# A transformer layer whose last three batches are projected beside the attention of the batch in front

## The reference

```
def bitnet_linear(x, weight, scale_param):
    s = jnp.maximum(jnp.mean(jnp.abs(weight), axis=1), 1e-08)
    y = jnp.einsum('bsi,oi->bso', x, jnp.sign(weight / s[:, None]))
    y = y * (s * scale_param)[None, None, :]
    return jnp.nan_to_num(y, nan=0.0, posinf=1000000.0, neginf=-1000000.0)
...
q, k, v = (bitnet_linear(layernorm(x), w, c) for w, c in ...)
attn = softmax(q @ k.T / sqrt(16)); x = x + bitnet_linear(attn @ v, o_weight, o_scale)
...
W = base + mean(abs(w - base)) * sign(w - base)     # for w1, w3 and w2
x = x + (silu(n @ W1.T) * (n @ W3.T)) @ W2.T        # n = layernorm(x)
```

## Time and profile before

| what | value |
|---|---|
| median of three runs | 1074.68 us |
| the profiled execution | 1078.31 us |
| its span, from the first to the last instruction | 1076.5 us |
| PE busy | 955.0 us (89%) |
| DVE busy | 784.5 us (73%) |
| ACT busy | 528.8 us (49%) |
| POOL busy | 132.8 us (12%) |
| mean granted clock of PE | 0.948 of 2.4 GHz |

### The profile page before, as it was taken

How to read it: one execution, slowest core, us unless ns; L and a number is a source line. 1 busy time by engine, 2 the same in 40 slices (tenths; PEclk the granted TensorE clock), 3 DMA queues, 4 the chain that set the end, 5 groups by cost and what they waited for, 6 DMA issues and landing times.

```text
span 1076.5 us, 14793 instructions
## 1 busy us (share of the span) xinstructions
PE 955.0 (89%) x4770; PEld 624.1 (58%) x4770; DVE 784.5 (73%) x1088; ACT 528.8 (49%) x972; POOL 132.8 (12%) x150
## 2 busy tenths in 40 slices
PE   1838348999999999997968999999999999999997
PEld 0727313333333333332445888888888888888886
DVE  6847468999999999996796557864588456864443
ACT  3624206888888888886556332232313332132221
POOL 0204001122111211110000111101101011011110
PEclk9978758999999999997889999999999999999999
DMA  7134324555456544634457200231002400040001
GB/s 253 35 101 164 117 100 122 179 147 145 131 168 170 140 142 143 183 80 142 138 159 238 68 1 1 66 114 60 0 0 78 161 0 0 9 147 1 0 0 39
DMA packets 78962, 106.06 MB, mean 99 GB/s; under 512 B 12960, under 2 KB 36512, under 8 KB 78912
## 3 DMA queue, kind: packets, MB, share of 16 engines
q1 hardware_dynamic: 75360, 101.04, 30.7%
q10 hardware_dynamic: 2688, 2.63, 0.7%
q0 software_dynamic: 864, 1.77, 0.5%
HBM read 76.29 MB, written 28.58 MB: 97 GB/s over the span
## 4 chain that ended last, share of the span: by engine, by line
PE 63%; DVE 14%; SPq 9%; DMA 8%; issue 4%; ACT 1%; POOL 0%; DVEq 0%; ACTq 0%
PE psum L1219 14%; PE psum L1220 14%; PE psum L1221 14%; DVE nmx L861 8%; PE psum L1133 6%; SPq L371 6%; PE psum L1123 6%; PE psum L1107 4%; DMA x_sb<-_attn_hidden_states_dram 2%; DMA factors<-wstat 2%; DVE dsum L947 2%; DMA q_parts<-q_lo 1%; PE psum L1144 1%; PE psum L1209 1%; PE psum L1145 1%
## 5 line engine op out<-in xcount | busy, mean ns | idle before, releaser
L687 ACT ACTIVATE probs<-psum 128x512 f32<-128x512 f32 x512 | 274.3, 602 | 92.5 <-PE psum L1123 91.5
L861 DVE TENSOR_REDUCE nmx<-psum 128x2 f32<-128x1024 f32 x256 | 300.4, 1218 | 26.3 <-PE psum L1107 24.2
L1219 PE MATMUL psum<-fxh,wh 128*128 128x512 f32 x448 | 175.2, 391 | 2.2 <-DVE wl L993 2.2
L1123 PE MATMUL psum<-q_slot,k_slot 50*128 50x512 f32 x512 | 160.4, 488 | 17.0 <-DMA q_slot<-shift 10.0
L1220 PE MATMUL psum<-fxl,wh 128*128 128x512 f32 x448 | 175.0, 391 | 0.0
L1221 PE MATMUL psum<-fxh,wl 128*128 128x512 f32 x448 | 174.8, 390 | 0.0
L1123 PEld LDWEIGHTS psum<-q_slot,k_slot 50*128 50x128 f32 x512 | 78.0, 190 | 135.5 <-ACT probs L687 101.1
L1133 PE MATMUL psum<-probs,v_slot 128*32 128x512 f32 x1024 | 140.7, 622 | 3.0 <-ACT probs L687 0.7
L1000 DVE TENSOR_TENSOR gate<-gate,psum 128x512 f32<-128x512 f32 x56 | 38.4, 686 | 133.8 <-PE psum L1221 131.5
L1107 PE MATMUL psum<-k_slot,q_slot 48*128 48x512 f32 x512 | 114.6, 460 | 9.6 <-DVE nmx L861 6.6
L745 ACT ACTIVATE hh<-gate 128x512 fp32r<-128x512 f32 x56 | 35.4, 632 | 162.6 <-DVE gate L1000 162.6
(11 more groups left out here) (102 smaller groups left out, 1148.1 us busy)
## 6 DMA issues: line engine op xcount, KB each, us to landing
stage<-in_L_ffn_mean_w_dram SPq DMA_DIRECT2D x84, 256.0 KB, 4.5
q_slot<-q_parts SPq DMA_DIRECT2D x174, 64.0 KB, 2.9
stage<-in_L_ffn_w_dram SPq DMA_DIRECT2D x42, 256.0 KB, 3.1
weighted_values<-u_sb SPq DMA_DIRECT2D x32, 256.0 KB, 2.2
k_slot<-k_stack SPq DMA_DIRECT2D x58, 96.0 KB, 2.7
x_sb<-_attn_hidden_states_dram SPq DMA_DIRECT2D x4, 1024.0 KB, 14.6
q_parts<-q_hi SPq DMA_DIRECT2D x32, 128.0 KB
q_parts<-q_lo SPq DMA_DIRECT2D x32, 128.0 KB
```

The lines of the kernel that those rows point to most:

```text
L687: nc.scalar.activation(probs[kt][:, j, :], BANK[ring_bank(("score", g, kt, j))], ACT.Exp, scale=HEAD_DIM ** -0.5).then_inc(exp_ok, 1)
L861: v.tensor_reduce(column, pair, AX.X, ALU.max, negate=True).then_inc(s_max, 1)
L1123: mm(BANK[ring_bank(("score", g, kt, j))], k_slot[s][rows, kt * P:(kt + 1) * P], q_slot[s][rows, jj, :], start=True, stop=True).then_inc(t ...
L1219: mm(o, lhs_hi, rhs_hi, start=first, stop=False)
```

## The change

Only batch 0 is projected up front. The projection of batch b+1 is written into the slices of batch b, by the place of the slice: the statistics of the tokens on DVE at places 0 to 4, the norm on GpSimd at 5, one transposed tile of tokens on PE at each of 8 to 11 (ACT evicts it, GpSimd splits it a slice later), one projected tile (an item, 8 matmuls) at 13, 15, 17, 19, 21 and 23, and the transposed values at 28. GpSimd clamps and masks an item one slice later, DVE selects and GpSimd splits it four slices later. SP stores it in the group that holds the sixth slice after it. What PE does beside the attention takes a bank of the same ring.

Three more things change. q is stored with its high part twice, so that a group is loaded by 4 DMAs and not 8. The sums of absolute differences leave DVE: ACT writes the absolute values (`ACT.Abs`), and GpSimd adds them to `dacc`, from which one reduction is taken at the end. The 14 tiles stand one to 8 slices, the first two loaded together ahead of group 0.

The diff, cut to its core:

```diff
+ITEMS = (KTILE, QT, QT + 1, QT + 2, QT + 3, VTILE)
+SLICES = KV_HEADS * TT
+STATS_AT, AGGR_AT, NORM_AT, XT_AT, SPLIT_AT = 0, 4, 5, 8, 9
+ITEM_AT = tuple(13 + 2 * i for i in range(len(ITEMS)))
+GUARD_LAG, PRED_LAG = 1, 4
+VT_AT = 28
+DIFF_AT = tuple(range(1, 112, 8))
+SIGN_LAG, ABS_LAG, SUM_LAG = 2, 5, 8
+Q_RING = 3
...
-    q_dram = nc.dram_tensor("q_parts", [GROUPS, 2, HEAD_DIM, REP, SEQ], FP32, kind="Internal").ap()
+    q_dram = nc.dram_tensor("q_stack", [GROUPS, REP, ROWS, SEQ], FP32, kind="Internal").ap()
...
-    SLOT_LOADS = 8 * 16
...
     def load_group(eng, g, s, done):
         for h in range(2):
-            rows = q_slot[s][HALF * h:HALF * h + ROWS].bitcast(FP32)
-            parts = q_dram[g, :, :, 2 * h:2 * h + 2, :]
-            for copy in range(2):
-                eng.dma_start(rows[HEAD_DIM * copy:HEAD_DIM * (copy + 1)], parts[0]).then_inc(done, 16)
-            eng.dma_start(rows[2 * HEAD_DIM:ROWS], parts[1]).then_inc(done, 16)
+            eng.dma_start(q_slot[s][HALF * h:HALF * h + ROWS].bitcast(FP32),
+                          q_dram[g, 2 * h:2 * h + 2].rearrange("j r t -> r j t")).then_inc(done, 16)
             eng.dma_start(k_slot[s][HALF * h:HALF * h + ROWS].bitcast(FP32), k_dram[g]).then_inc(done, 16)
+    def beside(g, kt):
+        b, at = g // KV_HEADS + 1, 4 * (g % KV_HEADS) + kt
+        if b == BATCH:
+            return None
+        if XT_AT <= at < XT_AT + KT:
+            return "xT", b, at - XT_AT
+        if at in ITEM_AT:
+            return "item", b, ITEM_AT.index(at)
+        if at == VT_AT:
+            return "vT", b
+        return None
...
+        def store_item(b, i):
+            c = 5 * b + i
+            m = ITEMS[i]
+            hi, lo = q_hi[c % Q_RING][:].bitcast(FP32), q_lo[c % Q_RING][:].bitcast(FP32)
+            g = KV_HEADS * b + 2 * m
+            def place(r):
+                if i == 0:
+                    return k_dram[KV_HEADS * b:KV_HEADS * (b + 1), r:r + HEAD_DIM, :]
+                return q_dram[g:g + 2, :, r:r + HEAD_DIM, :].rearrange("g j d t -> (g j) d t")
+            sp.wait_ge(qh_ok, c + 1)
+            sp.dma_start(place((0, HEAD_DIM)[i == 0]), hi).then_inc(part_out[c % Q_RING], 16)
+            sp.dma_start(place((HEAD_DIM, 2 * HEAD_DIM)[i == 0]), hi).then_inc(part_out[c % Q_RING], 16)
+            sp.wait_ge(ql_ok, c + 1)
+            sp.dma_start(place((2 * HEAD_DIM, 0)[i == 0]), lo).then_inc(part_out[c % Q_RING], 16)
...
+        load_tokens(0)
+        sp.wait_ge(w_in[1], 32)
+        sp.dma_start(w_nat[:, OT:, :], o_w.rearrange("(t p) c -> p t c", p=P)).then_inc(w_in[2], 16)
+        sp.wait_ge(xT_ok, KT)
+        load_tokens(1)
+        store_item(0, 0)
+        store_item(0, 1)
+        sp.wait_ge(slot_init, 10)
+        for g in range(2):
+            group_stored(g)
+            load_group(sp, g, g, slot_in[g])
+        store_item(0, 2)
+        store_item(0, 3)
+        store_item(0, 4)
+        group_stored(2)
+        load_group(sp, 2, 2, slot_in[2])
         sp.wait_ge(wstat_ok, 5)
         sp.dma_start(fac_dram.rearrange("a w p -> p a w"), wstat[:, 3:5, :],
                      allow_slow_non_contiguous=True).then_inc(fac_out, 16)
...
+        def load_difference(e):
+            if e >= 2:
+                sp.wait_ge(facc_ok, e - 1)
+                sp.wait_ge(fsgn_ok, 3 * (e - 1))
+            load_tile(e, wn[e % 2], (w1, w3, w2), fw_in[e % 2])
+            load_tile(e, mn[e % 2], (m1, m3, m2), fw_in[e % 2])
+        for e in range(2):
+            load_difference(e)
+        def sp_group(g):
+            b, at = divmod(4 * g, SLICES)
+            first, last = g == 0, g >= GROUPS - 4
+            s = g % 4
+            if b + 1 < BATCH:
+                for i in range(5):
+                    if at <= ITEM_AT[i] + 6 < at + 4:
+                        store_item(b + 1, i)
+            if g + 3 < GROUPS:
+                positive(sp, t_mm, 16 * g)
+                group_stored(g + 3)
+                load_group(sp, g + 3, (s + 3) % 4, slot_in[(s + 3) % 4])
+            if g < LAST_G:
+                load_shift(g + 1, (s + 1) % 4)
+            for e in range(2, IT):
+                if 4 * g - 2 < DIFF_AT[e - 2] + SUM_LAG + 1 <= 4 * g + 2:
+                    load_difference(e)
+            if b + 2 < BATCH and at == XT_AT + 4:
+                sp.wait_ge(xT_ok, KT * (b + 2))
+                load_tokens(b + 2)
...
+        def split_tokens(b, kt):
+            pool.wait_ge(xe_ok, 4 * (b - 1) + kt + 1)
+            if kt == 0:
+                pool.wait_ge(q_mm, NI * b)
+            nc.gpsimd.tensor_copy(xh[:, kt, :], xT[kt % 2][:]).then_inc(xh_ok, 1)
+            pool.wait_ge(xh_ok, 4 * b + kt + 1)
+            nc.gpsimd.tensor_tensor(xl[:, kt, :], xT[kt % 2][:], xh[:, kt, :].bitcast(FP32), ALU.subtract).then_inc(xl_ok, 1)
...
+        def difference(e):
+            pool.wait_ge(fw_in[e % 2], 96 * (e // 2 + 1))
+            nc.gpsimd.tensor_tensor(wn[e % 2][:], wn[e % 2][:], mn[e % 2][:], ALU.subtract).then_inc(fd_ok, 1)
+        def add_magnitude(e):
+            pool.wait_ge(fabs_ok, 3 * (e + 1))
+            positive(pool, facc_ok, e)
+            nc.gpsimd.tensor_tensor(dacc[:], dacc[:], mn[e % 2][:], ALU.add).then_inc(facc_ok, 1)
+        def pool_slice(g, kt):
+            b, at = g // KV_HEADS, 4 * (g % KV_HEADS) + kt
...
+            if b + 1 < BATCH:
+                if at == NORM_AT:
+                    norm_tokens(b + 1)
+                if SPLIT_AT <= at < SPLIT_AT + KT:
+                    split_tokens(b + 1, at - SPLIT_AT)
+                for i in range(NI):
+                    if at == ITEM_AT[i] + GUARD_LAG:
+                        guard_item(b + 1, i)
+                    if at == ITEM_AT[i] + PRED_LAG and i < 5:
+                        split_item(b + 1, i)
+            for e in range(IT):
+                if 4 * g + kt == DIFF_AT[e]:
+                    difference(e)
+                if 4 * g + kt == DIFF_AT[e] + SUM_LAG:
+                    add_magnitude(e)
...
+        def act_slice(g, kt):
+            for j in J_ORDER:
+                if j == J_ORDER[3]:
+                    if kt == 0 and g > 0:
+                        copy_u(g - 1)
+                    if beside(g, kt):
+                        beside_out(beside(g, kt))
...
+            for e in range(IT):
+                k = 4 * g + kt - DIFF_AT[e] - SIGN_LAG
+                if 0 <= k < 3:
+                    act.wait_ge(fd_ok, e + 1)
+                    nc.scalar.activation(sgn[:, e, k, :], wn[e % 2][:, k, :], ACT.Sign).then_inc(fsgn_ok, 1)
+                if 3 <= k < 6:
+                    nc.scalar.activation(mn[e % 2][:, k - 3, :], wn[e % 2][:, k - 3, :], ACT.Abs).then_inc(fabs_ok, 1)
...
+        def select_item(b, i):
+            n = NI * b + i
+            dve.wait_ge(mask_ok, 2 * n + 2)
+            settle(dve)
+            v.copy_predicated(g_alt[n % 2][:], g_mask[n % 2][:], yq[n % 2][:]).then_inc(yg_ok, 1)
...
+        def dve_slice(g, kt):
+            b, at = g // KV_HEADS, 4 * (g % KV_HEADS) + kt
+            n = 8 * g + 2 * kt + S_AHEAD
+            for a in range(2):
+                if n + a < S_USES:
+                    maxima(n + a)
+                if a == 0 and b + 1 < BATCH:
...
+                    for i in range(NI):
+                        if at == ITEM_AT[i] + PRED_LAG:
+                            select_item(b + 1, i)
+            if kt == 1 and g < LAST_G:
+                split_shift(g + 1)
...
+        def pe_slice(g, kt):
...
+            shifted_scores(g, kt, J_ORDER[0])
+            if n < S_USES:
+                scores(n)
+                scores(n + 1)
+            shifted_scores(g, kt, J_ORDER[1])
+            shifted_scores(g, kt, J_ORDER[2])
...
+            if kt == 1 and g < LAST_G:
+                transpose_maxima(g + 1)
+            if beside(g, kt):
+                beside_in(beside(g, kt))
+            shifted_scores(g, kt, J_ORDER[3])
```

712 lines of the change are left out of this document (335 added, 377 removed).

## The result

The changed kernel takes **1089.18 us** (median of 4 runs, 1086.45 to 1092.88) against 1074.2 us for the kernel before, measured beside it: a ratio of 1.0121 with a 95% interval of 1.0084 to 1.0157. It is **slower by about 13 us**. The forecast was 1065 us, faster.

The account below looks back on a forecast made before the run. No engine bounds the front, which ends with SP's waits; attention is close to full on PE and DVE. Front -78, attention +68 and +0.3 for the rest give -10 us: 1065 us, range 1035 to 1100.

Parts of the forecast that it names:

- The front: Before the first attention slice: it starts at 85.5 us against 163.5, 78 us less, bounds 72 to 102.
- Step 1: Plain attention slice: without DVE's reductions 2.66 us in place of 2.74, 2.7 us less per batch.
- Steps 2 to 4: Work added per batch: six items 12.0 us, token and value tiles 4.5, DVE's statistics, means and selects 3.3.
- step 4: DVE in a batch: four statistics, means and two selects in slices without an item add 3.3 us.
- Step 5: GpSimd: 66 us of work in over 100 a batch, no bound; selects held up by it cost 1 us a batch.
- Step 6: SP's list: PE waits for shifts at places 20, 24, 28, 3.3 us a batch, plus 1.3 of half clock.
- The rival with the late shift: SP's list, groups 4 to 6: stores ahead of the shift cause two more waits a batch, 44 us, 1109 us; chance 0.20.
- its condition: For the shift late in SP's list: GpSimd's clamp takes over 2.4 us, or a store over 2.5.
- The rival with locked-out selects: DVE at places 19 and 27: selects wait for GpSimd's wide operations, 5 us a batch more, 1080 us; chance 0.10.
- The rival in which the attention absorbs more: Attention: an item costs PE's 1.9 us less 0.5, no shift late; batches gain 42 us in all, 1039 us; chance 0.20.
- The signs named beforehand: First slice at 80 to 90 us; wrong if half clock inside batches 0 to 2, selects over 1.5 us, GpSimd over 90%.

Follow-up runs that it names:

- the late store: Changed kernel with the factors stored from ScalarE's queue in slice 6 and loaded by SP in group 7: ratio 1.0030, 10 us less.
- the short items: Kernel with DVE's masks (0.9910), items of batches 1 to 3 cut from eight matmuls to two: ratio 0.9832.
- Narrow operations: Changed kernel with GpSimd's differences and sums cut from 1,536 columns to 128: ratio 1.0006, 12 us less.
- The best version found: Changed kernel with wide operations moved, difference first, factors stored late, and item stores of batches 1 to 3 issued from GpSimd's queue: 1050.39 us, ratio 0.9746.
- the edit that gives the most: Item stores of batches 1 to 3 issued from GpSimd's queue, not SP's; alone on the changed kernel: ratio 1.0222, 11 us slower.

## Why the prediction was wrong

The sign was wrong; the time lies inside the range. By its steps:

- **The front: right.** -85 for -78; the first slice at 78.36 us for 85.5. The loads began at 42.4 us for 41. Two groups' loads took 3.7 us for 6, the nine stores behind them 10.1 for 14.4, the factors' store 14.3 for 16.6. That it was on the path is shown by the late store (-10 us). The bounds were not what their conditions give: stores at 1.8 us make 75 and a free factors' store makes 95, not 72 and 102.
- **Step 1, a plain slice: wrong by 2.7 us a batch.** Batch 3's groups take 10.98 us without DVE's reductions, and 10.8 and 11.2 by turns with them, the same on average. Taking work off DVE gave nothing.
- **Steps 2 to 4, the added work: right as a sum, partly by luck.** 15.27 against 10.98 for a group is 2.14 us an item, 2.0 taken; the short items show that it is PE's matmuls. But a tile cost 0.5 to 0.6 us (0.9 taken), and the group with the statistics is 0.8 us longer, where step 4 had 3.3. These errors and step 1's cancel: 16.3 us a batch, 17.1 forecast.
- **Step 5, GpSimd: it failed too, on the wait.** I priced the sum of its work (66 us; its own rows at 0.933 give 62, and the window shows 71) and asked if the batch could hold it. It could. The mask took 2.00 us for my 0.9 to 1.2, the norm 2.07 for 0.93. What counts is the latency at a place: 6.9 us of wide operations between two splits cost 4 us a batch at places 9 to 17, with half clock; the difference behind a sum makes ScalarE's sign wait at place 27; a select is held up to 3.7 us by the pair. I took 1 us a batch, 3 in all. Narrow operations take 10 us out of the three batches, and without the stores some 23 us stand at these two places.
- **Step 6, SP: this is the step that failed first.** Forecast were waits of 0.3, 0.3 and 2.7 us at places 20, 24 and 28 and 1.3 us of half clock, 14 us in all (by the step's own terms 12 - 11.9 leaves 0.1, not 0.3). Measured were 1.0 to 1.2, 2.1 to 2.5 and 3.6 to 5.8, with half clock behind four of the nine. The waits and slow clock that go with the stores are 21 us; what is left with narrow operations is 36. The list was right, item by item, and so was the shift (3.9 to 5.1 us for 3.95). The failed term is the loads: taken at 2 us for four, they held SP for 3.8 to 5.3 at places 20 and 28. At place 24 the wait for a store to land, up to 2.0 us, was not in the list. The six wide loads of the means were left out as well, but SP was through with them within 0.5 us of the next item's high part. By my own working groups 4 and 5 had no slack, and a sum without slack over four unmeasured terms is a forecast of a wait.

Over three batches the waits and slow clock came to 46 us, where steps 5 and 6 had 17. These 29 us are the error; the front gave 6.5 us more than forecast and the added work 2.4 less. How the 46 split between the two steps depends on which cause goes first, because one wait hides another: 21 to 36 us are the stores', 10 to 25 GpSimd's.

The rival with the late shift was the right mechanism, at 0.20. It said 44 us for two more waits a batch, on top of the forecast's 14; all three came in every batch, but most without half clock, and for 21 to 36 us. It came though its condition did not: the clamp and the mask, which the prediction counts as two clamps, took 0.67 and 2.00 us, neither over 2.4. The rival with locked-out selects was true in kind and in place: 2.5 us at place 19 in every batch and 3.3 once at 27, 8 us over a free select's time in all, where it had 15. The rival in which the attention absorbs more was false, by the short items.

The signs named beforehand told the truth: the first slice came in time, GpSimd was under 90%, but the clock was at half inside batches 0 to 2 and selects were over 1.5 us. The best version found keeps the change and takes 1050.39 us, 2.5% less than before.

## What to carry to other kernels

When work moves into a steady loop, write out each in-order list (SP's DMAs, GpSimd's) place by place with the waits in it, and ask what stands ahead of the item that the bound engine, or the engine that feeds it, needs; a list with no slack left should be forecast as late. Let whoever produces a tile store it, so that a wait for it holds up nobody else's transfers, but look first at what else that engine then runs beside, and at what then moves beside the small transfer that is waited for. And test causes together as well as alone: here the edit that gives the most costs time by itself.
